# A transformer block with a routed expert layer on one core: where GpSimd's late scatters and hand-outs stand, and a ring of 32 expert tiles instead of 16

## The reference

```python
x = x + _layernorm(attn_block(_layernorm(x)))     # 16 heads of 8, causal, relative bias; then relu(z W1) W2
h = _layernorm(x)
probs = softmax(h @ router_w.T); top_w, top_idx = top_k(probs, 2)
g = einsum('th,eih->tei', h, gate_w); u = einsum('th,eih->tei', h, up_w)
y = einsum('tei,ehi,te->th', silu(g) * u, down_w, w_te)      # w_te: top_w where chosen, else 0
x = x + _layernorm(y)
```

## Time and profile before

| | |
|---|---|
| time, median of 3 runs | 591.67 us |
| the three runs | 591.47, 597.71, 591.67 us |
| span of the profiled execution, first to last instruction | 596.4 us |
| the profiled execution's own time | not listed; 1.3 us above its span if it is the run of 597.71 |
| instructions | 14609 |
| PE busy | 532.1 us (89%) |
| DVE busy | 375.9 us (63%) |
| ACT busy | 395.4 us (66%) |
| POOL busy | 349.7 us (59%) |

### The profile page before, as it was taken

How to read it: one execution, slowest core, us unless ns; L and a number is a source line. 1 busy time by engine, 2 the same in 40 slices (tenths; PEclk the granted TensorE clock), 3 DMA queues, 4 the chain that set the end, 5 groups by cost and what they waited for, 6 DMA issues and landing times.

```text
span 596.4 us, 14609 instructions
## 1 busy us (share of the span) xinstructions
PE 532.1 (89%) x4952; PEld 395.0 (66%) x4969; DVE 375.9 (63%) x1095; ACT 395.4 (66%) x880; POOL 349.7 (59%) x449
## 2 busy tenths in 40 slices
PE   6989899899899899988899899999976899999981
PEld 5655455556566455655555666889976899999960
DVE  6824583965975947996847877527742365555347
ACT  3388989888978788869788696644531355555425
POOL 6104636545538885357877258487578555565545
PEclk9999999999999999999999999999996799999997
DMA  7245333213213322232734512212122203321174
GB/s 196 76 126 161 111 99 109 74 37 108 80 45 122 102 86 71 77 100 78 201 109 134 132 56 52 59 55 69 55 61 69 55 32 86 88 63 32 33 287 141
DMA packets 47016, 55.62 MB, mean 93 GB/s; under 512 B 7376, under 2 KB 41056, under 8 KB 44784
## 3 DMA queue, kind: packets, MB, share of 16 engines
q1 hardware_dynamic: 42624, 45.76, 26.7%
q0 software_dynamic: 4320, 8.92, 4.5%
HBM read 36.27 MB, written 18.92 MB: 93 GB/s over the span
## 4 chain that ended last, share of the span: by engine, by line
PE 56%; DVE 15%; ACT 10%; POOL 6%; issue 6%; DMA 3%; another core or an unknown queue 3%; DVEq 1%; SPq 0%; ACTq 0%; POOLq 0%
PE SC L871 11%; PE OA L748 9%; PE OA L881 6%; PE M L786 4%; PE M L822 4%; PE SC L730 3%; ACT arena L1015 3%; PE SC L734 2%; PE M L643 2%; DVE SS L1330 2%; PE SC L740 2%; PE M L662 1%; POOL slots L1782 1%; PE M L852 1%
## 5 line engine op out<-in xcount | busy, mean ns | idle before, releaser
L1015 ACT ACTIVATE arena<-SC 128x1024 f32<-128x1024 f32 x160 | 161.9, 1039 | 14.7 <-PE SC L735 11.8
L871 PE MATMUL SC<-arena 128*128 128x128 f32 (+1 forms) x852 | 111.5, 283 | 0.0
L871 PEld LDWEIGHTS SC<-arena 128*128 128x128 f32 (+1 forms) x852 | 104.0, 191 | 0.4 <-issue 0.3
L748 PE MATMUL OA<-arena 128*32 128x256 f32 (+1 forms) x1536 | 88.9, 349 | 6.6 <-DVE arena L455 2.8
L1782 POOL DMA_INDIRECT slots<-XBA,IDX x64 | 72.6, 1134 | 37.0 <-DVE IDX L1455 19.6
L1503 DVE TENSOR_TENSOR arena<-arena,SC 128x256 f32<-128x256 f32 (+1 forms) x142 | 43.7, 348 | 68.6 <-issue 24.6
L881 PE MATMUL OA<-arena 128*128 (+1 forms) x426 | 62.5, 284 | 12.9 <-issue 8.1
L748 PEld LDWEIGHTS OA<-arena 128*32 128x32 f32 x1536 | 39.2, 109 | 44.0 <-issue 22.8
L881 PEld LDWEIGHTS OA<-arena 128*128 128x128 f32 (+1 forms) x426 | 55.2, 198 | 15.4 <-issue 15.4
L454 POOL TENSOR_TENSOR arena<-arena 128x512 f32<-128x512 f32 x32 | 42.7, 1335 | 36.2 <-ACT arena L1015 35.6
L447 POOL TENSOR_TENSOR arena<-arena 128x512 f32<-128x512 f32 x23 | 31.2, 1356 | 48.9 <-ACT arena L1015 48.8
(11 more groups left out here) (244 smaller groups left out, 1086.0 us busy)
## 6 DMA issues: line engine op xcount, KB each, us to landing
arena<-parts SPq DMA_DIRECT2D x90, 192.0 KB
parts<-arena SPq DMA_DIRECT2D x16, 384.0 KB
arena<-ytok SPq DMA_DIRECT2D x8, 512.0 KB, 7.3
XGA<-slots SPq DMA_DIRECT2D x39, 65.0 KB
arena<-slots SPq DMA_DIRECT2D x32, 65.0 KB, 1.9
X<-in_L_attn_x SPq DMA_DIRECT2D x4, 512.0 KB, 5.1
out<-X SPq DMA_DIRECT2D x8, 256.0 KB, 2.5
arena<-parts SPq DMA_DIRECT2D x12, 96.0 KB
```

What stands on the lines that cost most here:

```text
L748: mm = pe.matmul(OA[32 * j:32 * j + 32, q0:q0 + n], vals[:, t, 32 * h:32 * h + 32], probs(j), start=first, stop=last, skip_group_check=True)
L871: mm = pe.matmul(SC[0:n, r % 2, 512 * m + P * c:512 * m + P * (c + 1)], WSEL[s % 4][:, I * m + i0:I * m + i0 + n], XGT[r % 2], start=True, ...
L1015: act.activation(EB[u], SC[:, n % 2, :], ACT.Exp).then_inc(exp_done, 1)
```

## The change

It touches GpSimd's order from body 8 on, and the ring. The 8 scatter DMAs of sequence 5 (`LATE5_AT`) stand one by one at positions 2, 4, ... 14 and 15 of body 8. The 16 of sequences 6 and 7 (`LATE67_AT`) stand one by one at positions 3 to 18 of body 9, that is at tiles 19 to 34. `handed_out(s)` says how many tiles have been handed out at tile s: all up to 19, then one for every four up to tile 34, and from there four for every three tiles until none is held. For this the ring has 32 buffers. The semaphores of the ring stay at 16 each (`MARKS`), so `load` and `put` wait in addition for the DMA that last used their semaphore.

```diff
-RING = 16
+RING = 32
...
-    dict(yroot=6, aroot=9, xroot=13, sc0=3, sc1=4, sc2=4, sc3=5, sc4=5, sc5=6, sc6=7, sc7=8))
+    dict(yroot=6, aroot=9, xroot=13))
+MARKS = 16
+LATE5_AT = (2, 4, 6, 8, 10, 12, 14, 15)
+LATE67_AT = tuple(range(3, 19))
+HELD = (19, 34)
...
+        def handed_out(s):
+            first, last = HELD
+            if s <= first:
+                return max(s, 0)
+            held = first + (min(s, last) - first) // 4
+            return min(s, held + max(s - last, 0) * 4 // 3)
...
                 if s >= RING:
-                    sp.wait_ge(ys_out[r], 16 * it)
-                sp.dma_start(XG[r][:, :], slots_d.ap()[bass.ds(row, P), :]).then_inc(xg_in[r], 16)
+                    sp.wait_ge(ys_out[s % MARKS], 16 * ((s - RING) // MARKS + 1))
+                if s >= MARKS:
+                    sp.wait_ge(xg_in[s % MARKS], 16 * (s // MARKS))
+                sp.dma_start(XG[r][:, :], slots_d.ap()[bass.ds(row, P), :]).then_inc(xg_in[s % MARKS], 16)
...
             def put(s, r):
                 pause()
+                if s >= MARKS:
+                    pool.wait_ge(ys_out[s % MARKS], 16 * (s // MARKS))
                 pool.wait_ge(ys_rdy, s + 1)
...
+                    if b == NB and n in LATE5_AT:
+                        scatter(NB - 3, LATE5_AT.index(n) // 2, (LATE5_AT.index(n) % 2,))
+                    if b == NB + 1 and n in LATE67_AT:
+                        i = LATE67_AT.index(n)
+                        scatter(NB - 2 + i // (2 * T), i // 2 % T, (i % 2,))
                     for s in early_tile(b, n):
-                        if s >= 1:
-                            put(s - 1, (s - 1) % RING)
+                        for k in range(handed_out(s - 1), handed_out(s)):
+                            put(k, k % RING)
```

More of the change, by code:

```diff
@@ L302, in block_kernel @@
         wt_full, wt_free = sem("wt_full"), sem("wt_free")
-        xg_in = [sem(f"xg_in{i}") for i in range(RING)]
+        xg_in = [sem(f"xg_in{i}") for i in range(MARKS)]
         xt_full, xt_rdy = sem("xt_full"), sem("xt_rdy")
@@ L307, in block_kernel @@
         y_full, ys_rdy = sem("y_full"), sem("ys_rdy")
-        ys_out = [sem(f"ys_out{i}") for i in range(RING)]
+        ys_out = [sem(f"ys_out{i}") for i in range(MARKS)]
         yt_in = [sem(f"yt_in{b}") for b in range(NB)]
@@ L583, in _, with load @@
                 stage(i)
-            def load(s, r, it):
+            def load(s, r):
                 row = sp.value_load(SRI[0:1, 0, s:s + 1], min_val=0, max_val=LAST_ROW)
@@ L604, in _ @@
                         sp.wait_ge(scattered[r], 16 * (NT - 2 * T))
-                load(s, s % RING, s // RING)
+                load(s, s % RING)
                 if s == PADS_AT:
@@ L616, in _ @@
             for s in range(EARLY, STILES):
-                load(s, s % RING, s // RING)
-            for r in range(RING):
-                sp.wait_ge(ys_out[r], 16 * len(range(r, STILES, RING)))
+                load(s, s % RING)
+            for r in range(MARKS):
+                sp.wait_ge(ys_out[r], 16 * len(range(r, STILES, MARKS)))
             yt_v = ytok_d.ap()[0:2 * NTOK, :].rearrange("(b p k t) d -> b p (k t d)", p=P, k=2, t=T)
@@ L853, in weights, with xt @@
                 mm.then_inc(wt_full, 1)
-            def xt(s, r, nload):
-                pe.wait_ge(xg_in[r % RING], nload)
+            def xt(s, r):
+                pe.wait_ge(xg_in[s % MARKS], 16 * (s // MARKS + 1))
                 pe.wait_ge(xt_rdy, s)
@@ L886, in woff, with step @@
                 return weights_offset(pe, s)
-            def step(s, r, it):
+            def step(s, r):
                 if s + 1 < STILES:
-                    xt(s + 1, r + 1, 16 * (it + 1 + (r + 1) // RING))
+                    xt(s + 1, r + 1)
                 if s < STILES:
@@ L908, in early @@
                     pe.wait_ge(table_rdy, 2)
-                step(s, s % RING, s // RING)
+                step(s, s % RING)
             pe.wait_ge(const_rdy, 1)
@@ L1766, in inv_root, with scatter @@
                 pool.tensor_tensor(RZ[:, k, :], RZ[:, k, :], MH[:, 0:T], ALU.pow).then_inc(done, 1)
-            def scatter(b, t):
+            def scatter(b, t, choices=(0, 1)):
                 r = b % 2
-                if t == 0:
+                if t == 0 and 0 in choices:
                     pool.wait_ge(xb2_rdy, b + 1)
@@ L1778, in scatter @@
                     pool.wait_ge(route_w, b // 2 + 1)
-                for k in range(2):
+                for k in choices:
                     if b >= NB - 4:
@@ L1794, in put @@
                                         out_offset=bass.IndirectOffsetOnAxis(ap=XG[r][:, D + 1:D + 2].bitcast(I32), axis=0),
-                                        in_=YS[r], in_offset=None).then_inc(ys_out[r], 16)
+                                        in_=YS[r], in_offset=None).then_inc(ys_out[s % MARKS], 16)
             far_values(0)
@@ L1826, in _ @@
                     for body in (b - 1, b):
-                        if body % 2 and body >= 3:
+                        if body % 2 and 3 <= body < NB:
                             for k in range(2 * T):
-                                if n + NU * (b - body) == POOL_AT[body >= NB][f"sc{k}"]:
+                                if (b < NB or k < T) and n + NU * (b - body) == PRE[f"sc{k}"]:
                                     scatter(body - 3 + k // T, k % T)
-                    for s in early_tile(b, n):
-                        if s >= 1:
-                            put(s - 1, (s - 1) % RING)
-            for s in range(EARLY - 1, STILES):
-                put(s, s % RING)
+                    if b == NB and n in LATE5_AT:
[3 more added lines that the diff above has]
+                        scatter(NB - 2 + i // (2 * T), i // 2 % T, (i % 2,))
+                    for s in early_tile(b, n):
+                        for k in range(handed_out(s - 1), handed_out(s)):
+                            put(k, k % RING)
+            for s in range(EARLY, STILES + 1):
+                for k in range(handed_out(s - 1), handed_out(s)):
+                    put(k, k % RING)
+            assert handed_out(STILES) == STILES
             def add_pair(b):
```

## The result

| | before | changed |
|---|---|---|
| median of 6 runs each, same lot | 592.21 us | 602.79 us |
| spread | 591.47 to 597.71 | 598.62 to 606.77 |
| the profiled execution, span | 596.4 us | 596.9 us |

The changed kernel takes 1.0149 of the time of the one before, with a 95% interval from 1.0095 to 1.0203: slower by 10.6 us. Its profiled execution is its fastest run (598.62), that of before is near its own slowest, so the two spans are almost the same. The profile therefore shows where things happen, but its sum can't be used for the difference of the medians.

A forecast was written before the change was run, and what follows sets the result against it. PE was taken to bound the expert tiles, except from 433 to 468 us, where its signals seemed late. Terms 0 + 5.8 + 1.8 + 0 = +7.6 on 591.67 gave 599.3 us; range 582 to 605, the forecast's own 596 to 603.

The forecast's parts named there:

- The new wait: Body 8, n = 15: VectorE's `XBA` step waits for sequence 5's last scatter, leaving PE idle at `down(15)`; +5.8 us.
- The clock: Just behind PE's idle time at tile 15: granted clock falls to 1.2 GHz for half a tile or more; +1.8 us.
- The late row: Bodies 8/9, tiles 19 on: scatters still go at 1.46 us, not one per tile; 0, bounds -17.7 to +7.
- the 17.7 us: Time above PE's own pace estimated in five slow tile steps from 440.09 to 468.35 us of the earlier profile.
- The reading behind it: Stretch 433 to 468 us: GpSimd's long unbroken issuing of computed-address DMAs coincides with late PE completion signals; some 17.7 us.
- The sign of being wrong: Tiles 19 on: scatters 1.46 us apart while PE runs at 2.11 us a tile would show the row doesn't delay PE.
- The earlier row: Body 8, n = 2 to 9: spreading the eight scatters removes a small lag but leaves GpSimd fewer gaps; 0, -1 to +3.
- Loads and stores: SP's loads 16 to 39 and eight `pads` pieces go earlier or one behind the other, with nobody waiting; 0 us.
- the covered wait: Tiles 14 to 17: GpSimd issues its last scatter early or PE has slack; -1 to +3, about 592.5 us; chance 0.08.
- the fours of scatters: Tiles 19 to 25: scatters in fours lengthen PE's delay; +7 with two more slow tiles, 606.4 us; chance 0.17.
- rival 1: Slow stretch 433 to 468 us vanishes, caused by SP's loads and pads or put/scatter order; -10.1, 581.6 us; chance 0.25.
- The base: The whole kernel: +7.6 us is added to the earlier median 591.67, not to the profile's span of 596.4; gives 599.3.

The follow-up runs named there:

- lot 4: Fourth group of runs, on one chip, kernel before at 580.8 us: the changed kernel unaltered (587.06 us, 1.0146), and a version with earlier scatters and longer pauses (1.0073).
- lot 2: Second group of runs, on one chip, kernel before at 597.5 us: parts of the change run separately, and one version with DMAs waiting for tiles; ratios 0.9890 to 1.0112.
- spread scatters alone: The kernel before with only the scatters of sequence 5 spread over positions 2 to 15 of body 8: 604.51 us, ratio 1.0112.
- late part alone: The changed kernel with the scatters of sequence 5 back in their row at body 8, n = 2 and 3: 599.26 us, ratio 1.0029.
- lot 3: Third group of runs, on one chip, kernel before at 580.1 us: four altered versions, ratios 0.9962 to 1.0203.
- pacing: Late scatters and puts each also wait for the tile before their own: 0.9890 on the late part alone, 0.9951 on the early list.
- lot 1: First group of runs, on one chip: the kernel before at 592.2 us and the changed kernel at 602.8 us, ratio 1.0149.
- lot 5: Fifth group of runs, on one chip, kernel before at 592.3 us: sequence 5's scatters early (1.0012), and the same with late DMAs waiting for tiles (0.9951).
- early list: The changed kernel with the scatters of sequence 5 one per tile at tiles 2 to 9: 577.18 us (0.9962), on another chip 593.11 us (1.0012).
- row paced: The late part alone, with only sequence 6 and 7 scatters and held-stretch puts waiting for the tile before; catch-up puts go freely: 580.11 us, ratio 0.9993.
- ring alone: The kernel before with only the ring of 32 and its earlier loads, order unchanged: 599.49 us, ratio 1.0041.

## Why the prediction was right, and where not

**The new wait (+5.8 forecast).** Right in mechanism, place and nearly in size. The last scatter started at 424.49, forecast 423.7; VectorE went on at 426.92, forecast 426.1; from the start of a scatter to the step behind it took 2.43 us, forecast 2.4 (the Trainium skill's estimate of 2.15, from "DMA: Bandwidth & Descriptors", is 0.28 short). PE's idle time was 5.94 us. The waiting instruction was named wrongly: it was not `down(15)` behind `hidden(15)` but `rx` (L842), which turns `XBA` itself and stands on PE's list three places earlier, ahead of `xt(17)` and `gu(16)`. That the size came out is in part luck, for the faults nearly cancelled. The forecast counted the `select` and `hidden` behind `XBA`, which PE didn't have to wait for (0.52 + 0.62). It had VectorE going on 0.8 us too early. And it let PE's idle time begin with `down(15)` at 422.59, while before the change PE stood at `rx` at 420.71, 1.9 us earlier; this was made up for by the changed kernel's profile being later as a whole there (its first tile is done at 381.29, before at 379.81), so that PE came to `rx` at 422.2.

**The clock (+1.8 forecast).** With the wait the whole step is +8.0 against 5.8 + 1.8 = 7.6. The `gu` behind took 2.77 us in place of 1.49, at the lower level for half a tile to a tile. In lot 4, where PE was idle for 7.01 us, the step is +9.6; in lot 2, with the spread scatters alone, 10.70 - 2.55 = +8.2. So this sum of two terms, the only ones not at zero, held within 2 us on three chips.

**The late row (0 forecast).** Right in value: the late part alone is 1.0029 on a chip with late signals, and on the quiet chip of lot 3 the late loss with it is 1.5 us. Right also that "a list is no clock": the scatters went at 1.46 to 1.8 us. The copies 5 to 6 us apart that should have shown it did not come: the changed profile has steps of 2.1 to 4.4 us there. The bounds were too generous on the gain side, since they let the 17.7 us hang on this change.

**The reading behind it** was half wrong, and the coincidence it was drawn from could not have shown it. "While GpSimd issues computed-address DMAs without a pause for long, PE's completion signals arrive late" holds on the chips of lots 2 and 5 (pacing takes 15 to 16 us of late loss away in both) and, by the look of its profile, on that of lot 1. It does not hold on those of lots 3 and 4, where the same instructions at the same pitch cost 1.5 to 1.8 us. The sign of being wrong, "if they stand at 1.46 and PE runs on at 2.11 a tile", is what came there. The rule weighed against it, that DMA never contends with a compute engine and that PE and ACT never wait on anyone ("SBUF — State Buffer" of the Trainium skill, "Who interferes with whom"), fits lots 3 and 4. In lots 2 and 5 ScalarE does wait, 4.08 us ahead of the copy of 457.10 in lot 5, and PE behind it. The section speaks of ports of the SBUF, and what comes late is a signal, so the rule isn't contradicted in its own words.

**The earlier row (0, from -1 to +3).** Spread or early, it was a small gain, larger than the one us allowed. In lot 3 the early list reaches tile 18 at 432.3, the row of before at 435.4 at the earliest (row paced), both on the same chip; 1.6 of the 3.1 us are in the step of tile 18 (4.82 against 6.43; three of the seven profiles with the old row have 4.8 there too). What is left of it in the medians is 0.9962. The spread list won as much on the quiet chip of lot 4: against the row-paced profile of lot 3 the steps from tile 0 to 14 take 1.3 us less and those from 15 to 19 another 1.65. That is about what makes +6.3 us in the time out of a step of +9.6. On chips with late signals the lag that was allowed for did come: tile 12 took 4.45 us in the changed kernel and 4.59 with the spread scatters alone, against 2.11 in lot 4.

**Loads and stores (0).** Right for the ring: 1.0041 in itself. The rival in which SP's loads and stores cause the bad stretch (0.25 with its fellows) is not settled by the identical pair of lots 3 and 5, since GpSimd and SP both do the same in it. It falls with the ring alone (the loads freed, 21.1 us still lost) and with pacing in lot 2, where SP's stores stayed in their place and the loss went from 19.1 to 3.4 us. The stores were moved by themselves only on a quiet chip, so that they have a share in it isn't ruled out. Of the others, the covered wait falls with VectorE's 6.72 us, and the fours of scatters with lot 2: the late part alone loses 19.1 us, the order of before (ring alone) 21.1, where +7 was priced for the fours. In the chances behind the range, four fifths of rival 1's 0.25 are 0.20, not the 0.22 put there.

**The base.** Adding 7.6 to the median of three runs gave 599.3; 602.79 was measured, the difference against the six runs being 10.6. The surplus of 3 us is within the noise: the interval of the ratio is 5.6 to 12.0 us, six runs of before spread over 6.2 us, six of the changed kernel over 8.2. What else is in the 10.6 is not shown; the one profile of each kernel can't tell, since their late losses differ by 8.6 us the other way.

**What stays open.** What differs between the chips (or between the times at which they were measured), and by which mechanism GpSimd's DMAs make a signal late. Also why on a chip with late signals a piece of the row goes clean (tiles 24 to 28 of the changed kernel, DMAs 1.5 to 1.8 us apart) while three puts at 1.46 and 1.54 us delay a signal elsewhere. In the changed kernel's profile the mean pitch is the same over slow and clean tiles (1.61 us from 444.69 to 459.16, with tiles of 3.3 to 4.3 us, and 1.62 from there to 468.89), so within this narrow range it doesn't decide; no run with a longer pitch landed on such a chip. That the signal is late and not the work is read from PE's rows: `xt` and `gu` follow the `down` of 452.32 without a gap in lot 5. The ends of PE's rows are modelled by the profile.

**Is there a better version?** The changed kernel with the early list beats both on a quiet chip (0.9962), and with pacing it is at 0.9951 on a chip with late signals. These are gains under 1%; the late part with pacing, 0.9890, is the largest seen, and at 1.1% also just at what a measurement of this kernel can tell. On a quiet chip the paced versions were only tried in part (0.9993).

## What to carry to other kernels

When work is moved later, look for who reuses its buffer: the cost of this change was one wait that its spread-out scatters put into VectorE's way, found by asking what must have landed before `XBA` may be written. A DMA moved onto another position keeps its pace unless something makes it wait. And a loss whose main label is "remote" should be seen on a second chip before a kernel is reordered for it; here it was 18.2 us on one chip and 1.5 on another, for the same instructions.

## What the runs showed of the hardware

- The same kernel took 577.2 us on one chip and 593.1 on another (its own spreads 576.8 to 581.1 and 589.0 to 600.1). The kernel before took 580.1, 580.8, 592.2, 592.3 and 597.5 in five lots.
- That difference of 15.9 us stands nearly all in one place: late loss 1.5 against 18.2 us, in a stretch in which GpSimd issues computed-address DMAs mostly 1.46 to 1.8 us apart. There PE's completions reach ScalarE and VectorE late: a copy starts 3.85 us after the end of its `down` in lot 5, 4.50 us before the change, 7.55 us with the spread scatters alone (`down` ends at 470.99, its copy starts at 478.54). The profile calls most of that idle time "remote".
- On such a chip three computed-address DMAs in a row went with a signal 2.0 us late; waiting for a tile between them took most of the late loss away (19.1 to 3.4 us, 18.2 to 3.5 us).
- Slower issuing is no free remedy: a second memset ahead of each such DMA left GpSimd 6.5 and 7.4 us behind at the end, against 1.1.
